# A recurrence step in a four-layer block: its decay on GpSimd, a scan over three elements into SBUF, a PSUM bank passed on

## The reference

```python
x = x + _L0_cond_ref(x, cond, ...)      # experts, 128 -> 128
x = x + _L1_cond_ref(x, cond, ...)      # experts
x = x + _L2_cond_ref(cond, x, W, b, alpha)
x = x + _L3_cond_ref(x, cond, mask, ...)

def step(h, z_t):                       # _L2, scanned over 256 positions; leak = 1 - alpha
    gate = jax.nn.sigmoid(h @ Wh.T + z_t @ Wz.T + b)
    h_new = jnp.tanh(h * leak + gate * z_t)
    return (h_new, h_new)
```

## Time and profile before

| | before |
|---|---|
| median of 3 runs | 498.97 us (496.51 to 498.99) |
| the profiled execution | 497.72 us, its span 495.9 us |
| granted TensorE clock, mean | 0.993 |
| busy: PE, DVE, ACT, POOL | 93%, 64%, 54%, 7% |
| DMA, mean over the span | 17 GB/s |

### The profile page before, as it was taken

The page is one execution under the profiler, slowest core; times in us unless marked ns, Lnnn a source line. Parts: engine busy times, 40 slices in busy tenths (PEclk is TensorE's granted clock), DMA queues, the critical chain, the costliest instruction groups (busy, mean ns, idle before and its releaser), DMA issues.

```text
span 495.9 us, 13421 instructions
## 1 busy us (share of the span) xinstructions
PE 463.6 (93%) x4657; PEld 326.4 (66%) x4657; DVE 318.3 (64%) x1197; ACT 265.9 (54%) x881; POOL 32.5 (7%) x108
## 2 busy tenths in 40 slices
PE   3899999899999999999999999999999998999994
PEld 2678687568777677787767777566645664555662
DVE  6856787777776766777877775677458736016641
ACT  3453635533645556636434456743684468864562
POOL 7210201200110201101010010000000000000000
PEclk9999999899999999999999999999999999999998
DMA  8500000000000000000000000000010001001001
GB/s 304 216 1 2 2 1 1 3 1 1 3 1 1 1 3 0 2 3 1 1 1 3 2 2 0 3 2 2 4 23 2 4 1 23 4 4 23 3 3 23
DMA packets 7985, 8.41 MB, mean 17 GB/s; under 512 B 5616, under 2 KB 6896, under 8 KB 7792
## 3 DMA queue, kind: packets, MB, share of 16 engines
q1 hardware_dynamic: 7488, 7.29, 4.5%
q10 hardware_dynamic: 432, 0.27, 0.2%
HBM read 6.44 MB, written 1.05 MB: 15 GB/s over the span
## 4 chain that ended last, share of the span: by engine, by line
PE 77%; ACT 11%; DVE 5%; issue 3%; DMA 2%; POOL 1%; ACTq 0%; SPq 0%; DVEq 0%
PE ybk L982 17%; PE hid L1127 13%; PE cbk L1147 11%; PE ybk L1103 6%; PE cbk L1151 3%; ACT hb L830 3%; PE hid L968 3%; PE hid L1079 3%; DVE vbk L1456 2%; PE hid L1032 2%; ACT d L904 2%; PE cbk L1079 2%; PE hid L1014 1%; PE hid L1035 1%; PE hid L1084 1%
## 5 line engine op out<-in xcount | busy, mean ns | idle before, releaser
L1147 PEld LDWEIGHTS cbk<-hs,rec 128*128 128x128 f32 x512 | 77.4, 189 | 50.1 <-ACT hs L908 35.0
L982 PE MATMUL ybk<-hg,down 128*128 128x256 f32 x352 | 95.6, 397 | 0.9 <-DVE hg L1333 0.5
L1147 PE MATMUL cbk<-hs,rec 128*128 128x8 f32 x512 | 90.5, 249 | 6.2 <-ACT hs L908 2.1
L1127 PE MATMUL hid<-xsp,up 128*128 128x256 f16 x672 | 92.9, 279 | 3.3 <-DVE lg L1277 0.9
L1456 DVE TENSOR_TENSOR_SCAN vbk<-d 128x16 f32<-128x16 f32 x256 | 51.4, 201 | 63.5 <-ACT d L904 59.5
L904 ACT ACTIVATE d<-cbk 128x8 f32<-128x8 f32 x256 | 45.6, 178 | 73.1 <-PE cbk L1147 72.3
L908 ACT ACTIVATE hs<-vbk 128x8 f32<-128x8 f32 x256 | 45.4, 178 | 64.6 <-DVE vbk L1456 63.0
L1127 PEld LDWEIGHTS hid<-xsp,up 128*128 128x128 f16 x672 | 63.3, 105 | 14.6 <-ACT hb L830 2.8
L1451 DVE SCALAR_TENSOR_TENSOR d<-hs,leak,d 128x8 f32<-128x8 f32 x256 | 56.9, 222 | 13.2 <-ACT hs L908 12.9
L982 PEld LDWEIGHTS ybk<-hg,down 128*128 128x128 f32 x352 | 60.5, 191 | 7.0 <-DVE hg L1333 1.0
L1338 DVE TENSOR_TENSOR hg<-hb,hid 128x512 f32<-128x512 f32 x64 | 43.7, 686 | 1.9 <-PE hid L968 1.6
(11 more groups left out here) (186 smaller groups left out, 630.0 us busy)
## 6 DMA issues: line engine op xcount, KB each, us to landing
qz<-up_in SPq DMA_DIRECT2D x3, 512.0 KB, 7.6
kp<-maskr_in SPq DMA_DIRECT2D x1, 1024.0 KB, 11.6
out_dram<-silu SPq DMA_DIRECT2D x4, 256.0 KB, 3.0
x<-x_in SPq DMA_DIRECT2D x7, 128.0 KB, 8.8
down<-down_in SPq DMA_DIRECT2D x1, 768.0 KB, 9.6
att<-att_in SPq DMA_DIRECT2D x1, 751.0 KB, 9.9
down<-down_in SPq DMA_DIRECT2D x1, 640.0 KB, 6.8
qz<-rows SPq DMA_DIRECT2D x32, 2.0 KB, 1.7
```

The source lines that it names most:

```text
L982: m = pe.matmul(ybk[l][:, 0:n], D(l, "w2" if shared else "e2", e * f + i), hg[:, hg_of[made] % NHG, i * n:i * n + n], start=first and i == ...
L1127: m = pe.matmul(into, up[:, pw, a:a + P], x_part(c, l, px, slice(0, n)), start=j == 0, stop=j == 2)
L1147: pe.matmul(cbk[c % 2][:, o:o + B], wh, hs[:, t, :], start=False, stop=True, skip_group_check=True).then_inc(gate_pre, 1)
```

## The change

- `DECAY` moves from DVE to GpSimd and computes only `h * leak`, a `tensor_tensor` of 128x8 elements with `leak` broadcast. Each waits for its NEW (`h_full`), and SCAN waits for it (`decay`), as before.
- `SCAN` runs over three elements for each sequence, 24 in all: (0, th), (z/2, z/2), (1, h * leak). The three lie in one SBUF tensor `dd` of 64 positions (`ZR`) in place of `d0` and `d1`. It now waits for Z itself.
- `SCAN` writes to SBUF (`vps` is an SBUF tensor of 24 columns), and `NEW` reads every third of these from SBUF.
- `vbk` carries no scan any more and becomes a fourth bank for units during the recurrence: `NHT` 4, `TAIL` 2.
- `Z` is two ACT instructions of 256 elements for a chunk in place of one, since z/2 is needed as factor and as addend.
- RG's six GpSimd instructions are placed one by one, between DECAYs.
- The planner's assumed step goes from 1.15 to 1.11 us, DECAY is no longer reserved on DVE, and the window of DVE goes from 0.68 to 0.88 us; GpSimd gets a window like the others.

```diff
-ZR = 128
-NHT, NHB, NHG = 3, 8, 4
-TAIL = 3
+ZR = 64
+NHT, NHB, NHG = 4, 8, 4
+TAIL = 2
...
-SLACK = {"pe": .1, "act": .05, "dve": .05, "pool": 9.}
-WINDOW = {"pe": .88, "act": .45, "dve": .68, "pool": 9.}
+SLACK = {"pe": .1, "act": .05, "dve": .05, "pool": .1}
+WINDOW = {"pe": .88, "act": .45, "dve": .88, "pool": .88}
...
-        scan = gate + .23 if kind in ("STEP", "GATE") else at
-        new = scan + .25 if kind != "NEW" else at
-        ready = new + .24
+        scan = gate + .22 if kind in ("STEP", "GATE") else at
+        new = scan + .24 if kind != "NEW" else at
+        ready = new + .22
...
+        if kind != "DECAY":
+            soon["pool"] = new + .23
...
-            soon["dve"] = ready + .66 - .24
+            soon["dve"] = ready + .66
...
-            if kind == "DECAY":
-                soon["dve"] = max(soon["dve"] + .24, free[eng] + .05)
-            else:
+            if kind != "DECAY":
                 last[eng] = kind, free[eng]
                 foresee(key, at)
...
-        d0 = sb("d0", [P, ZR, B, 2])
-        d1 = sb("d1", [P, 2, B, 2])
+        dd = sb("dd", [P, ZR, 2, B, 3])
...
-        hid = [ps(f"hid{i}") for i in range(NHT)] + [vbk] + cbk
-        vps = vbk[:, 0:2 * B]
+        hid = [ps(f"hid{i}") for i in range(NHT - 1)] + [vbk] + cbk
+        vps = sb("vps", [P, 3 * B])
...
+                if kind == "DECAY":
+
+                    t, = key
+                    if t:
+                        pool.wait_ge(h_full, t)
+                    else:
+                        pool.wait_ge(in_rec, 32)
+                        pool.wait_ge(consts, 1)
+                    tts(dd[:, t % ZR, 1, :, 2], hs[:, t, :], leak[:, 0:1].broadcast_to([P, B]), ALU.mult).then_inc(decay, 1)
...
-            new = vps.rearrange("p (b o) -> p b o", o=2)[:, :, 1]
+            new = vps[:].rearrange("p (b o) -> p b o", o=3)[:, :, 2]
...
-                    dve.wait_ge(act_done, nth["act", ("Z", chunk_of(t))])
-                    stt(d1[:, t % 2, :, 1], hs[:, t, :], leak[:], d0[:, t % ZR, :, 1], ALU.mult, ALU.add).then_inc(decay, 1)
-                elif key[0] == "SCAN":
+                if key[0] == "SCAN":
                     t = key[1]
                     dve.wait_ge(gate_th, t + 1)
                     dve.wait_ge(decay, t + 1)
-                    nc.vector.tensor_tensor_scan(vps, d0[:, t % ZR].rearrange("p b o -> p (b o)"),
-                                                 d1[:, t % 2].rearrange("p b o -> p (b o)"), 0.0, ALU.mult,
+                    dve.wait_ge(act_done, nth["act", ("Z", chunk_of(t))])
+                    nc.vector.tensor_tensor_scan(vps[:], dd[:, t % ZR, 0].rearrange("p b o -> p (b o)"),
+                                                 dd[:, t % ZR, 1].rearrange("p b o -> p (b o)"), 0.0, ALU.mult,
                                                  ALU.add).then_inc(blend, 1)
```

More of the change, by code:

```diff
@@ L130, in costs @@
         "TR": {"pe": (.25,), "dve": (.42,)}, "O": {"pe": (.86,), "dve": (.75,)},
-        "STEP": {"pe": (.22,)}, "GATE": {"act": (.18,)}, "SCAN": {"dve": (.2,)}, "NEW": {"act": (.18,)}, "DECAY": {"dve": (.22,)},
+        "STEP": {"pe": (.22,)}, "GATE": {"act": (.18,)}, "SCAN": {"dve": (.2,)}, "NEW": {"act": (.18,)}, "DECAY": {"pool": (.25,)},
     }[k]
@@ L157, in schedule @@
         needs[key] = [(k, of, next(iter(costs(key)))) for k, of in {
-            "DECAY": [(("Z", c), "act")] + before_t, "STEP": [(("C", c), "pe")] + before_t, "GATE": [(("STEP", t), "pe")],
-            "SCAN": [(("GATE", t), "act"), (("DECAY", t), "dve")], "NEW": [(("SCAN", t), "dve")]}[kind]]
+            "DECAY": before_t, "STEP": [(("C", c), "pe")] + before_t, "GATE": [(("STEP", t), "pe")],
+            "SCAN": [(("GATE", t), "act"), (("DECAY", t), "pool"), (("Z", c), "act")], "NEW": [(("SCAN", t), "dve")]}[kind]]
     for key in chain + [u[0] for u in units]:
@@ L173, in schedule @@
     hb_at, hg_at = {}, {}
-    open_at = {NHT: ("NEW", T - 1), NHT + 1: ("NEW", T - 1), NHT + 2: ("NEW", T - 1)}
+    open_at = {NHT: ("NEW", T - 1), NHT + 1: ("NEW", T - 1)}
     def bank():
@@ L193, in start @@
         mine = costs(key)
-        hop = .08 if number[key] >= 0 else .05
+        hop = .08 if number[key] >= 0 else .04
         for e in ENGINES[:ENGINES.index(eng)]:
@@ L721, in link @@
                 ins.then_inc(pool_link, 1)
-                pool.wait_ge(pool_link, chain[0])
             tts, tsc = nc.gpsimd.tensor_tensor, nc.gpsimd.tensor_scalar
-            for (kind, *key), _ in lists["pool"]:
-                if kind == "RG":
+            for (kind, *key), part in lists["pool"]:
+                if kind == "DECAY":
[6 more added lines that the diff above has]
+                    tts(dd[:, t % ZR, 1, :, 2], hs[:, t, :], leak[:, 0:1].broadcast_to([P, B]), ALU.mult).then_inc(decay, 1)
+                else:
@@ new lines, in _ @@
+                    if part == 0:
+                        pool.wait_ge(dve_done, nth["dve", ("RC", c, l)])
+                        if c:
+                            pool.wait_ge(pe_done, nth["pe", ("GT", c - 1, l)])
+                        if nth["pool", ("RG", c, l)] > 1:
+                            pool.wait_ge(gates_made, nth["pool", ("RG", c, l)] - 1)
+                    else:
+                        pool.wait_ge(pool_link, chain[0])
+                    if part == 0:
+                        link(tts(pick[:, l, 0:k, :], both[:, l, 0:k, 0, :], both[:, l, 0:k, 1, :], ALU.add))
+                    elif part == 1:
+                        link(tts(gr[:, 0:k, :], sg[:, l, 0:k, :], wide(rcp2[:, l, 0:k]), ALU.mult))
+                    elif part == 2:
+                        link(tts(gr[:, 0:k, :], gr[:, 0:k, :], wide(zer2[:, l, 0:k]), ALU.add))
+                    elif part == 3:
+                        link(tts(gr[:, 0:k, :], gr[:, 0:k, :], pick[:, l, 0:k, :], ALU.mult))
+                    elif part == 4:
+                        link(nc.gpsimd.tensor_copy(g2[:, l, 0:k, 0:E], gr[:, 0:k, :]))
+                    else:
+                        tts(g2[:, l, 0:k, E:2 * E], gr[:, 0:k, :], g2[:, l, 0:k, 0:E], ALU.subtract).then_inc(gates_made, 1)
@@ L780, in unit @@
                     z0 = STARTS[c] % ZR
-                    nc.scalar.activation(d0[:, z0:z0 + CHUNKS[c], :, 1], x[:, cols(c)].rearrange("p (t b) -> p t b", b=B),
-                                         ACT.Copy, scale=0.5).then_inc(act_done, 1)
+                    i = nc.scalar.activation(dd[:, z0:z0 + CHUNKS[c], part, :, 1], x[:, cols(c)].rearrange("p (t b) -> p t b", b=B),
+                                             ACT.Copy, scale=0.5)
+                    if part:
+                        i.then_inc(act_done, 1)
                 elif kind == "MB":
@@ L903, in _ @@
                     act.wait_ge(gate_pre, t + 1)
-                    nc.scalar.activation(d1[:, t % 2, :, 0], cbk[c % 2][:, o:o + B], ACT.Tanh, scale=0.5).then_inc(gate_th, 1)
+                    nc.scalar.activation(dd[:, t % ZR, 1, :, 0], cbk[c % 2][:, o:o + B], ACT.Tanh, scale=0.5).then_inc(gate_th, 1)
                 elif key[0] == "NEW":
```

24 lines of the change are left out of this document (4 added, 20 removed).

## The result

The changed kernel takes 493.1 us (492.9 to 493.8, 4 runs) against 498.6 us of the kernel before: a ratio of 0.989, 95% interval 0.987 to 0.992. In a second series (e11) the ratio was 0.990 (0.985 to 0.994). The forecast was 492. Executions over 1.5% longer than the fastest of their kernel, which had a mean granted TensorE clock of 0.975 to 0.979, are left out of all medians, ranges and intervals here. Its profiled execution took 493.16 us, with a span of 491.4, against 497.72 and 495.9 before.

What follows compares the result with a forecast made beforehand. The chain at its 1.10 us floor was taken to set most recurrence steps, PE some steps and the last part. 497.72 + 4.9 (step) - 2 (chunk 1) - 9 (bank) = 491.6, said as 492; 478 to 506, about 8 in 10.

Steps and rivals of the forecast that it cites:

- NEW, +30 ns forecast: NEW on ACT reads SBUF in place of PSUM: 208 ns against 178, +30 ns in each step, on the chain.
- SCAN, +7 ns forecast: DVE scan of 24 elements to SBUF: +7 ns at 0.93 ns an element, between 27 less and 24 more.
- The step, 1.137 forecast: Recurrence step from NEW to NEW: 1.100 + 0.030 + 0.007 = 1.137 us, between 1.103 and 1.154.
- Absorption, half of it: Of 9.5 us from longer steps, chunk 2's wait swallows 2.4 and steps set by PE 2.2; recurrence grows 4.9.
- DECAY off DVE, -2 us in chunk 1: 56.9 us of DVE time go; the room lets chunk 1's late expert layers gain 2 us, between 0 and 5.
- The fourth bank, -9 us: Units replace fillers in the recurrence: 7 us from steps with six, 2 from those with fewer; bounds zero and 25.
- rival 1: The step grows and the bank doesn't fill, as DVE's pace rules: 501 us, or 504; chance 0.24 in both forms.
- DECAY on GpSimd, no cost: DECAY on GpSimd ends 0.39 us before SCAN is due, which covers one RG instruction ahead; cost zero.
- Rival 3: DECAY comes late, GpSimd blocked by DVE instructions with two SBUF inputs: 495.5 us; chance 0.10.
- rival 2: The scan gets shorter off PSUM, step 1.103 us: 487.5 us; chance 0.12.
- rival 4: The fourth bank fills most of the filler time, 22 us of it: 478 us; chance 0.10.
- The signs: Profile after: NEW 205 to 212 ns, SCAN 200 to 212, step 1.13 to 1.145 us, last part under 140 us.

Runs made afterwards that it cites:

- e11: The changed kernel run once more, unaltered, in a later series; 493.5 us, ratio 0.990 to the kernel before.
- e1: The changed kernel with three unit banks during the recurrence (NHT 3, TAIL 3) in place of four; 504.0 us, ratio 1.011.
- e2: e1 with the same instruction lists, but the 24-element scan writes to its old PSUM bank and NEW reads there; 498.1 us, ratio 1.000.
- e9: The changed kernel with a fourth scan element per sequence (factor 1, addend 0; 32 elements, SBUF), same lists and result; 499.3 us, ratio 1.003.
- e13: e3 with a 16-element scan; GpSimd makes h * leak, then adds z/2 in a second instruction; Z is one instruction; 488.1 us, ratio 0.979.
- e12: e3 run once more, unaltered, in the same series as e10, e11 and e13; 490.5 us, ratio 0.985.
- e4: The kernel before with only vbk as fourth unit bank and its 16-element scan in unused cbk columns; DECAY stays on DVE; 495.9 us, ratio 0.997.
- e3: The changed kernel, same lists and four banks, but the scan writes to 24 unused columns of the PSUM bank cbk; 490.2 us, ratio 0.985.
- e10: e3 with a dummy instruction of the old DECAY's shape on DVE ahead of each SCAN, lists and banks unchanged; 491.5 us, ratio 0.986.
- e5: The changed kernel with the planner's assumed step of 1.15 us and engine hop of 0.05 us as before; 493.8 us, ratio 0.992.

## Why the prediction was right

The time was right to 1.1 us, the direction too. Term by term it was less exact, and part of the hit is luck.

The forecast took 6.1 us off a profiled execution whose trace has a stretch at half the clock in chunk 1. Rows 2 show it, as 0.96, and the prediction read all of that chunk's 11.8 us as lateness. At an equal clock the gain is about 3 us, half of what was forecast. Put together from the runs, as an estimate at an equal clock: the longer step costs 9 us (three quarters of 12.0, forecast 4.9); the bank brings 8 (e1 to the changed kernel, forecast 9); DECAY off DVE with the planner's settings brings some 4.5 (e2 has the time of before, within 1 us, with a step longer by 21 ns, of which three quarters are 4.0; forecast 2). That sums to 3.5. The step's cost was put too low by 4 us. What hid that was the room on DVE, put too low too, and the clock.

- **NEW, +30 ns forecast.** +35 measured (213 ns, just above the 205 to 212 that I named). The mechanism, an ACT read of SBUF against PSUM, is shown by e2: same lists, PSUM, 178 ns. The Trainium skill's difference (Perfetto Trace Analysis, section Optimizing Scalar/DVE Operations, 93 against 51 ns) is 42; the runs lie between my rows and it.
- **SCAN, +7 ns forecast.** +8 measured, by chance. Two terms were wrong. An element costs the scan 2.1 to 2.2 ns (e9, and before to e2), not the 0.93 of a plain instruction, so eight cost 17 to 18 (the Trainium skill has this, in DVE: opcode table, instruction layouts, handler registers and perf-mode slots, section Datapath and trigger behaviour: the built-in scan "runs at half throughput"; the runs agree, and the prediction did not use it); and leaving PSUM gave back 9 to 10, which stood only in the lower bound, at 27. By the Trainium skill's figures for DVE (Perfetto Trace Analysis, section Optimizing Scalar/DVE Operations, about 60 ns on SBUF and 125 on PSUM) it would be an estimated 65 ns; the direction holds and the size doesn't for this scan, which reads SBUF and only writes PSUM: 219 against 209 ns (e2 and changed).
- **GATE, not priced.** +4 ns. With the output two elements apart (e13) it is 177 to 178, with three 182, with four 185 (from three to four, in e9, nothing but the distance changed). I had not looked at the changed stride.
- **The step, 1.137 forecast.** 1.147, within 1.103 to 1.154: 12.0 us over 256 steps in place of 9.5.
- **Absorption, half of it.** This term was mis-sized: a quarter is absorbed. I let steps set by PE and the wait for chunk 2 swallow 4.6 of 9.5 us. With lists held equal and over stretches at the full clock, the recurrence answers to 3.1 of 4.1 us (e1, e2), 4.2 of 5.1 (e9) and 5.3 of 7.2 (e12), and the whole time at the higher clock to about 5 of 6.7, 5.8 of 5.9 and 4.4 of 7.2. My reading, which no run isolates: a step in which PE is late is late by its list of units, and that list stays behind the STEP that starts it; it only absorbs if the gap is long enough.
- **DECAY off DVE, -2 us in chunk 1.** Chunk 1 became 6.1 us shorter. The wait between its last step and the next is the larger part: from NEW to NEW it was 7.9 us and is 3.7. But about 1.7 of the 6.1 is the clock. In the trace of before PE sat idle for most of 94 to 96 us and then had 1.2 GHz for 3.4 us, from 96.3 (the last number but two is the granted clock):

```profile
94.00:96.00 2.00, 0.52 (x6) 0.26 (x4) 1.59 (x6) 0.84 (x3) 1.55 (x4) 1.00 0.00 0
96.00:98.00 2.00, 1.90 (x12) 1.39 (x12) 1.00 (x4) 0.72 (x3) 0.00 (x0) 0.58 0.02 4
```

  In after, NEW at 117.99, C at 120.02 and STEP at 120.80:

```profile
117.99 0.21 ACT L927 ACTIVATE hs<-vps 128x8 f32<-128x8 f32 x1 [0.27 <-DVE vps L1468]
118.23 0.61 DVE L1275 TENSOR_TENSOR x<-x,hs 128x256 f32<-128x256 f32 x1 [0.28 <-ACT hs L927]
118.28 0.51 POOL L733 TENSOR_TENSOR dd<-hs,leak 128x8 f32<-128x8 f32 x1 [0.94 <-ACT hs L927]
...
120.02 0.59 PE L1012 MATMUL cbk<-x,rec 128*128 128x256 f32 x2
...
120.80 0.30 PEld L1166 LDWEIGHTS cbk<-hs,rec 128*128 128x128 f32 x2
```

  In e4 that distance is 3.7 us too with DECAY on DVE, in e1 it is 6.1 with DECAY on GpSimd. Counted from the first STEP, C of chunk 2 starts at 81.5 us in before (79.8 without the 1.7), 79.3 in e1, 78.1 in e2, 77.4 in after and 75.5 in e4. So the bank alone brings chunk 2 at least as early as both together, and the change without it brings it forward by 0.5 to 1.7 us. I had given all of it to the room on DVE.
- **The fourth bank, -9 us.** The tail gave 5.6, and the rest came where I had not put it, in the recurrence: all that it lost over 256 floors fell from 24.7 to 15.0 us, 1.7 of that by the clock. Steps with six fillers went from 19 to 13 only, but fillers from 222 to 146. With an equal step the bank is worth 7.9 us (e2, e3) or 10.8 (e1, changed) between medians, 6 to 7 or 8 at the higher clock. The reason that I gave, no bank open in 13 steps, is half of it: with DECAY on DVE the bank is worth 1.9 (e4). The argument of rival 1 was sound as to e4, where DVE's plan is full; it missed that the change takes that limit away at the same time. e10 shows that what counts most is where the planner may put units. That a unit's bank is held until DVE gets to it, and that this links the two parts, is my reading; no run isolates it.
- **DECAY on GpSimd, no cost.** Right. It starts 0.29 us behind NEW (0.24 forecast; the hop to GpSimd is 76 ns, not 30) and ends 0.41 us before SCAN in the median step (0.39 forecast). GATE to SCAN rose by 3 ns. Rival 3's mechanism shows in the rows above: at 118.23 DVE starts an instruction with two SBUF inputs, and the DECAY of 118.28 takes 0.51 us in place of 0.21. In nine of 256 steps it took 0.34 to 0.85 us, and in one, step 47, it ended behind GATE. There DVE's own long instruction held SCAN until 98.15, and DECAY, at 98.21, for 0.06 us more:

```profile
96.95 1.20 DVE L1416 TENSOR_TENSOR kq<-small,vimg 128x1024 f32<-128x1024 f32 x1
...
97.36 0.85 POOL L733 TENSOR_TENSOR dd<-hs,leak 128x8 f32<-128x8 f32 x1 [0.94 <-ACT hs L927]
...
97.77 0.18 ACT L923 ACTIVATE dd<-cbk 128x8 f32<-128x8 f32 x1
...
98.30 0.21 DVE L1468 TENSOR_TENSOR_SCAN vps<-dd 128x24 f32<-128x24 f32 x1
```

- **Rivals.** The slower one is what e1 is: it would have been right without the fourth bank. The shorter step (rival 2) and the late DECAY (rival 3) did not come; the bank filling most (rival 4) came to a third.
- **The signs.** SCAN, the fillers, GATE to SCAN and the recurrence were as named. Three missed by little: NEW 213 ns (205 to 212 named), the step 1.147 us (up to 1.145), the last part 140.2 us (under 140).

## What to carry to other kernels

When a serial chain and bulk work share the engines, price a change to the chain at its number of steps times the change in the median step, with a small discount at most: here three quarters to four fifths of it reached the end of the recurrence. The same lists with one memory exchanged (e1 and e2) give that price cleanly, if stretches at the same granted clock are compared. A second resource may be worth little alone and much with the first: the fourth bank brought 1.9 us, taking DECAY off DVE with a longer step brought nothing (e2), both together 7.6 (e3). And before a gain of 1% is split into terms, look whether the trace of before holds a stretch at the lower clock: here it was 1.7 us of what seemed lateness. Last, before a buffer is moved from PSUM to SBUF to free its bank, look for unused columns in a bank that the chain holds anyway: that kept the bank and the fast read, and gave another 3 us.

## What the runs showed of the hardware

- ACT reads 8 elements in 178 ns from PSUM and 213 from SBUF; the DVE scan is the other way round, 219 ns with its output in PSUM and 209 in SBUF for 24 elements.
- The DVE scan takes 2.1 to 2.2 ns an element where a plain DVE instruction takes 0.93.
- An ACT instruction writing 8 elements to SBUF takes 178, 182 and 185 ns with steps of two, three and four elements.
- A GpSimd tensor_tensor of 8 elements takes 203 to 205 ns in the median and up to 0.85 us beside a DVE instruction with two SBUF inputs (step 47 of the changed kernel), and starts 76 ns behind the end of the ACT instruction that it waits for, where SCAN on DVE starts 33 behind GATE's.
- Executions of one kernel differ by the clock that PE was granted: the kernel before took 496.0 us at 0.997, 498.2 at 0.993 and 500.9 at 0.984 in one series. In e5's profile the drop is one piece. PE was busy for 1.69 of 2 us from 80 to 82, full before that, and then had the lower of its two levels, 1.2 GHz (0.50), for some ten us:

```profile
80.00:82.00 2.00, 1.69 (x16) 1.36 (x16) 1.39 (x7) 0.81 (x4) 0.41 (x2) 1.00 0.00 0
82.00:84.00 2.00, 2.00 (x14) 1.41 (x14) 1.14 (x5) 1.10 (x5) 0.26 (x1) 0.61 0.00 0
84.00:86.00 2.00, 2.00 (x16) 1.55 (x15) 0.99 (x8) 0.89 (x5) 0.30 (x2) 0.50 0.00 0
```

  The changed kernel has similar stretches (1.65 of 2 us busy from 84 to 86) and kept the full clock there. What decides it, no run here shows; differences of 1 to 2 us between medians are within this spread. In the profiles of e9, e10 and e11 such a stretch is 13.7 to 17.1 us long and starts at 346 to 348 us.
